# Threshold search of a gated attention block: eight tiles of marks divided anew among ScalarE, VectorE and GpSimd

## What is computed

```python
sim = jnp.einsum('bhnd,bhmd->bnm', Q, K) / (jnp.sqrt(jnp.float32(d)) * H)
k = max(1, int(n * TOP_K_RATIO))                 # 153 of 512
threshold = jax.lax.top_k(sim, k)[0][:, :, -1:]
sparse_mask = (sim >= threshold).astype(sim.dtype)
A_learned = jax.nn.sigmoid(sim) * sparse_mask
A_learned = (A_learned + jnp.swapaxes(A_learned, -1, -2)) * 0.5
x = x + tanh(g_xattn[0]) * ((1.0 - gamma) * layernorm(x) + gamma * A_learned)
```

## Time and profile before

| what | value |
|---|---|
| median of three runs | 1872.8 us (1871.12 to 1873.93) |
| the profiled execution's own time | 1870.53 us |
| its span, first to last instruction | 1868.7 us |
| busy in the span: PE, DVE, ACT, POOL | 1484.8, 1112.7, 980.8, 635.6 us |
| the threshold search | from 41 to about 347 us of the span |

### The profile page before, as it was taken

One profiled execution on the slowest core, in us unless ns is written; L12 is line 12 of the kernel. 1 busy time (PEld: TensorE's weight loads), 2 busy tenths in 40 slices (PEclk: granted clock), 3 DMA queues, 4 the chain that ended last, 5 costly groups with the idle time before them and its releaser, 6 DMA issues. The chain is left out here.

```text
span 1868.7 us, 31243 instructions
## 1 busy us (share of the span) xinstructions
PE 1484.8 (79%) x10376; PEld 777.9 (42%) x10395; DVE 1112.7 (60%) x1785; ACT 980.8 (52%) x1503; POOL 635.6 (34%) x557
## 2 busy tenths in 40 slices
PE   6666666677776775999999711899999999999994
PEld 2444455543333332444444310444444444444442
DVE  3999999788888896888886472205415140541000
ACT  4999999733232233777777440344444444444442
POOL 3000000010000000788888535435445444544432
PEclk9778777788898897999999765999999999999998
DMA  9311100000000000000000256315335151531113
GB/s 336 135 46 46 46 1 1 29 1 1 0 0 0 0 0 1 3 2 3 2 3 3 88 190 249 117 35 163 111 86 168 26 165 34 163 95 34 30 28 102
DMA packets 49246, 118.69 MB, mean 64 GB/s; under 512 B 5536, under 2 KB 5792, under 8 KB 48576
## 3 DMA queue, kind: packets, MB, share of 16 engines
q1 hardware_dynamic: 34832, 88.53, 14.0%
q0 software_dynamic: 8176, 18.65, 5.1%
q10 hardware_dynamic: 6144, 10.28, 1.8%
HBM read 84.21 MB, written 37.43 MB: 65 GB/s over the span
## 5 line engine op out<-in xcount | busy, mean ns | idle before, releaser
L1622 PE MATMUL PS<-R 128*128 (+1 forms) x1872 | 432.7, 381 | 8.3 <-issue 7.2
L1776 DVE TENSOR_SCALAR R<-wring 128x1024 f16<-128x1024 f32 x56 | 61.5, 1108 | 382.6 <-PE PS L1645 349.2
L425 ACT ACTIVATE R<-R 128x512 bf16<-128x512 f32 x448 | 278.9, 715 | 9.4 <-PE PS L445 3.9
L1622 PEld LDWEIGHTS PS<-R 128*128 128x128 f16 x1872 | 179.5, 98 | 217.6 <-issue 19.7
L445 PE MATMUL PS<-R,ident_b 128*128 128x256 bf16 (+1 forms) x1056 | 168.6, 321 | 83.1 <-ACT R L425 79.1
L1645 PE MATMUL PS<-R 128*128 (+1 forms) x936 | 214.8, 379 | 1.2 <-ACT R L1732 1.2
L1812 POOL TENSOR_TENSOR R<-R 128x512 f32<-128x512 f32 x78 | 113.3, 1453 | 292.0 <-ACT R L1720 181.0
L871 PE MATMUL PS<-R 128*128 128x512 bf16 x495 | 141.9, 436 | 78.6 <-DVE R L807 60.4
L1036 DVE TENSOR_REDUCE R<-PS 128x1 f32<-128x512 f32 x256 | 166.6, 686 | 45.2 <-PE PS L1218 42.6
L1014 POOL TENSOR_TENSOR R<-R 128x512 f32<-128x512 f32 x128 | 166.6, 1302 | 27.8 <-ACT R L1141 12.2
L1141 ACT ACTIVATE R<-PS 128x512 f32<-128x512 f32 x256 | 144.4, 598 | 41.3 <-PE PS L1232 40.8
(11 more groups left out here) (262 smaller groups left out, 2522.3 us busy)
## 6 DMA issues: line engine op xcount, KB each, us to landing
wring<-in_L_ffn_w_kernel_dram SPq DMA_DIRECT2D x48, 512.0 KB, 5.3
slot_rows<-R SPq DMA_DIRECT2D x1, 10023.0 KB, 40.3
R<-slot_rows ACTq DMA_DIRECT2D x39, 257.0 KB, 2.7
R<-in_L_ffn_w_kernel_dram SPq DMA_DIRECT2D x16, 512.0 KB, 5.6
wring<-in_L_ffn_wo_kernel_dram SPq DMA_DIRECT2D x16, 512.0 KB, 4.5
R<-in_L_ffn_wo_kernel_dram SPq DMA_DIRECT2D x16, 512.0 KB, 4.7
X<-in_x_dram SPq DMA_DIRECT2D x4, 1024.0 KB, 9.0
R<-in_L_ffn_w_up_dram SPq DMA_DIRECT2D x4, 1024.0 KB, 10.3
```

The costliest lines, as they stand in the source:

```text
L425: nc.scalar.activation(marks[:, j * S:(j + 1) * S], SIM[:, tile * S:(tile + 1) * S], ACT.Sign, bias=cfloat[:, tile:tile + 1], scale=-1.0). ...
L1622: mm = nc.tensor.matmul(bank[2 * half + g], ZT[n][:, (4 * pz + k) * P:(4 * pz + k + 1) * P], weights(place, at), start=(i % 12 == 0), stop ...
```

## The change

ACT makes six of the eight tiles of marks, POOL the last two (`POOL_MARKS = 2`), DVE none. POOL's loop `pool_search` takes the place of `pool_linear`: in each half it waits for the candidates and for the last fold of the half before, marks two tiles, and in every fourth half also does one of the 16 tiles of the linear update. PE's doubled fold covers tiles 6 and 7 and waits for POOL's count; the plain one covers tiles 4 and 5. Two small DVE steps, keep (L513) and near (L536), are written with two tensors as inputs: the constant -1 comes from a new tensor `minus` of 128 x 8 set once by a memset, and the bit, one value per row, is broadcast over the eight columns. The two counting halves behind the search keep their marks on DVE, with the semaphore's counts adapted.

```diff
-ACT_MARKS = 7
+ACT_MARKS = 6
+POOL_MARKS = 2
...
+        minus = R3[:, 5944:5952]
...
                         pe.wait_ge(marked, h * ACT_MARKS + (ACT_MARKS if q else 4))
                         if q:
-                            pe.wait_ge(marked_dve, h + 1)
+                            pe.wait_ge(marked_pool, (h + 1) * POOL_MARKS)
                     else:
-                        pe.wait_ge(marked_dve, HALVES + (h - HALVES) * HALF + 4 * q + 4)
+                        pe.wait_ge(marked_dve, (h - HALVES) * HALF + 4 * q + 4)
                     if q and h < HALVES:
-                        fold((7, 8), ident_2)
-                        mm = fold((4, 7), ident_b[:])
+                        fold((ACT_MARKS, 8), ident_2)
+                        mm = fold((4, ACT_MARKS), ident_b[:])
...
+            nc.vector.memset(minus, -1.0).then_inc(bit_step, 1)
...
-            def mark(h):
-                t = h % 2 * HALF + HALF - 1
-                v.wait_ge(cand_ready, h + 1)
-                if h:
-                    v.wait_ge(fold_ps, 2 * h)
-                nc.vector.tensor_scalar(marks[:, (HALF - 1) * S:], SIM[:, t * S:(t + 1) * S], cfloat[:, t:t + 1], 0.5,
-                                        ALU.is_lt, ALU.subtract).then_inc(marked_dve, 1)
-
...
-                nc.vector.tensor_scalar(keep[:, g], cnt[:, g], float(S - 2 * TOPK), -1.0, ALU.is_le,
-                                        ALU.mult).then_inc(keep_step, 1)
+                nc.vector.scalar_tensor_tensor(out=keep[:, g], in0=cnt[:, g], scalar=float(S - 2 * TOPK), in1=minus,
+                                               op0=ALU.is_le, op1=ALU.mult).then_inc(keep_step, 1)
...
-                    nc.vector.tensor_scalar(near[:, g], key[:, g], bit[:, n + 2:n + 3], None,
+                    nc.vector.tensor_tensor(near[:, g], key[:, g], bit[:, n + 2:n + 3].broadcast_to([P, HALF]),
                                             ALU.bitwise_xor).then_inc(near_step, 1)
...
-            mark(0)
             for u in range(12):
                 for k in range(5):
-                    mark(5 * u + k + 1)
                     search(5 * u + k)
                     dve_weights(v, u, k)
...
-        def pool_linear(pool):
-
-            pool.wait_ge(coef_ready, 5)
-            for t in range(NT):
-                xt = X[:, t * D:(t + 1) * D]
-                nc.gpsimd.tensor_scalar(xt, xt, s1[:, t:t + 1], s2[:, t:t + 1], ALU.mult, ALU.add).then_inc(lin, 1)
+        def pool_search(pool):
+            pool.wait_ge(sim_sb, NT)
+            for h in range(HALVES):
+                pool.wait_ge(cand_ready, h + 1)
+                if h:
+                    pool.wait_ge(fold_ps, 2 * h)
+                for j in range(ACT_MARKS, HALF):
+                    tile = h % 2 * HALF + j
+                    nc.gpsimd.tensor_scalar(marks[:, j * S:(j + 1) * S], SIM[:, tile * S:(tile + 1) * S],
+                                            cfloat[:, tile:tile + 1], 0.5, ALU.is_lt, ALU.subtract).then_inc(marked_pool, 1)
+                if h % 4 == 3:
+                    t = h // 4
+                    if t == 0:
+                        pool.wait_ge(coef_ready, 5)
+                    xt = X[:, t * D:(t + 1) * D]
+                    nc.gpsimd.tensor_scalar(xt, xt, s1[:, t:t + 1], s2[:, t:t + 1], ALU.mult, ALU.add).then_inc(lin, 1)
```

More of the change, by code:

```diff
@@ L97, in bass_flamingo @@
         ln_step = sem("ln_step"); bit_step = sem("bit_step"); cand_ready = sem("cand_ready")
-        marked = sem("marked"); marked_dve = sem("marked_dve"); tallied = sem("tallied"); keep_step = sem("keep_step"); key_step = sem("key_step"); near_step = sem("near_step"); fold_ps = sem("fold_ps"); fin_step = sem("fin_step")
+        marked = sem("marked"); marked_dve = sem("marked_dve"); marked_pool = sem("marked_pool"); tallied = sem("tallied"); keep_step = sem("keep_step"); key_step = sem("key_step"); near_step = sem("near_step"); fold_ps = sem("fold_ps"); fin_step = sem("fin_step")
         tg_ready = sem("tg_ready")
@@ L486, in dve_a @@
             nc.vector.memset(cbits, 0).then_inc(bit_step, 1)
+            nc.vector.memset(minus, -1.0).then_inc(bit_step, 1)
             for n in range(32):
                 nc.vector.memset(bit[:, n:n + 1], -2 ** 31 if n == 0 else 2 ** (31 - n)).then_inc(bit_step, 1)
-            v.wait_ge(bit_step, 35)
+            v.wait_ge(bit_step, 36)
             v.wait_ge(id_ready, 2)
@@ L492, in dve_a @@
             nc.vector.tensor_scalar(ident_2, ident_b[:], 2.0, None, ALU.mult).then_inc(bit_step, 1)
-            v.wait_ge(bit_step, 36)
+            v.wait_ge(bit_step, 37)
             nc.vector.tensor_copy(gone, key).then_inc(cand_ready, 2)
@@ L547, in dve_a @@
             for h in range(60, HALVES):
-                if h + 1 < HALVES:
-                    mark(h + 1)
                 search(h)
@@ L1868, in _ @@
             pool_ln(pool, 0)
-            pool_linear(pool)
+            pool_search(pool)
             pool_b_weights(pool)
```

## The result

The changed kernel takes 2036.9 us against 1872.0: 1.0879 times as long (95% interval 1.0845 to 1.0913), 165 us more. One of the four executions of the changed kernel was slow as a whole (2234.4 us at a granted clock of 0.75) and the ratio leaves it out; the other three took 2032.9 to 2038.4. The kernel before was timed anew beside each group of experiments, with medians from 1872.0 to 1874.5, and each ratio is taken against those times. The forecast had the sign right and nothing else: 1898, with a range of 1860 to 1920.

What follows compares the result with a forecast made beforehand. ACT and DVE, both full, bound the search at 23.9 us a round. DVE's 21.9 plus 4.4 lost to POOL gives 26.3, +28.9 over twelve rounds; less gains at the ends, net +25.4: 1898 us, range 1860 to 1920.

Steps and rivals of the forecast that it cites:

- Part 1 and 2: Search: ACT loses one mark of seven, 3.1 us a round, to 20.8; DVE loses its mark, 2.0, to 21.9.
- Part 3: Small DVE steps (L513, L536) rewritten with two tensors as inputs: same cost, together nothing.
- Part 4, first term: POOL's marks in the search priced at 0.76 us each; with the updates 8.5 us a round.
- signs of being wrong: Closing list: the prediction would be wrong if the marks' instruction is far from 0.76, or DVE comes to wait for folds.
- Part 4, who waits: Search: DVE steps with SBUF inputs and POOL instructions take turns; DVE's loss makes the round 26.3 us against 23.9.
- The loss of 4.4 us: DVE's time lost a round of the search to POOL's marks and updates, between bounds of 2.1 and 7.0.
- lower bound of 2.1: DVE's loss a round if everything that can hide does: 6.4 of POOL's 8.5 us covered by tallies, reduction and reciprocal.
- the placing half by half: POOL's marks placed in each half of a round: DVE losses of 0.15, 2.2 and 1.4 us, plus 0.65 for the update.
- Rival 3: POOL starves behind DVE's train of instructions; mark and fold come on top, 10.6 us a round, 1972 us; chance 0.06.
- 2.0 x 12 + 3.5: Sum of the rival with no blocking to speak of between POOL and DVE: 27.3 us less, 1845.5; chance 0.05.

Runs made afterwards that it cites:

- pool_fast: The changed kernel with POOL's marks computed as mult and add in place of less-than and subtract (not the reference's result): 1868.9 us, 0.9967 of before.
- act7_pool1: The changed kernel with seven tiles of marks on ACT, one on POOL and none on DVE: 1871.0 us, 0.9988 of before.
- narrow_weights: The changed kernel with DVE's weight steps on 64 of each unit's 2048 columns (not the reference's result): 1939.3 us, 1.0354 of before.
- linear_alone: The kernel before with only POOL's linear update moved into the search, one tile every fourth half: 1873.7 us, 0.9995 of before.
- forms: The kernel before plus six POOL instructions of 128x512 while POOL and DVE are idle: mult+add 0.69 and 0.70 us, less-than+subtract 2.02 and 2.00.
- forms2: The kernel before plus six further POOL instructions of 128x512 to bf16 while POOL and DVE are idle: mult alone took 1.57 us.

## Why the prediction was wrong

- **Part 1 and 2** (ACT 20.8, DVE 21.9 us a round; relief of one is worth nothing) fit what was measured: in pool_fast DVE sets the round, in act7_pool1 ACT does, at its 23.9.
- **Part 3** holds: nothing within what can be measured.
- **Part 4, first term: the step that failed.** "The nearest row is the linear update itself, one input, 512 elements, 0.76 us; I take it for the marks." Same engine, same shape, same number of tensor inputs, but another pair of operations: 2.0 us. The price was given without a second end, though the trace had no POOL instruction with this pair; that a mark far from 0.76 would break the sum stands only among the signs of being wrong, with no time worked out for it. With 2.0 the forecast's own fold and the hand-over of 0.13 seen since give the loop: 0.13 + 4.0 + 1.94 is 6.1 us a half before any waiting, against 4.8 available. This loop of marks and fold was never worked out; with 0.76 it would have been 3.6 and harmless.
- **Part 4, who waits.** The sum lets DVE pay for each meeting. In the changed kernel it is POOL that pays: in four halves of five the second mark falls behind one of DVE's long steps and takes 1.5 to 1.8 us more, and in one of them (the half with L721) the first mark is 0.97 longer as well; as POOL is on the loop, everybody waits. narrow_weights puts 98 us on DVE's long steps, some 90 of them on this wait. Which DVE instructions hold POOL's up and which don't was placed rightly (long steps do, tally and reduction don't); that POOL's hold up DVE's two-input steps came true for marks of 0.70 us (L525) and not for those of 2.0.
- **The loss of 4.4 us** with marks of the assumed price was too high as well: 1.7, under the lower bound of 2.1. DVE loses mostly at the candidates (L525, 0.22 a half on average), and little at its long steps, because a mark released in a long step waits until its end and then runs beside the tally, as linear_alone shows with the update alone. The bound of 2.1 had 11.25 x 0.76 in it; with the 0.70 of the pair to bf16 the same sum gives 11.25 x 0.70 - 6.4 = 1.5, and 1.7 lies just above it. What was too high is the step from the bound to 4.4, the placing half by half.
- **Rival 3** (POOL starves, mark and fold on top, 1972) comes nearest in mechanism: POOL does wait for DVE and PE for POOL. It had the loop, but reached it by starvation alone and with the wrong mark. It had 0.06. Two of the rivals' sums are slightly off: 4 x 2.7 is 10.8 a round and not 10.6, which gives rival 3 about 1975, and 2.0 x 12 + 3.5 is 27.5 and not 27.3.
- **The Trainium skill** (SBUF — State Buffer, Who interferes with whom) was right that DVE's two-input steps and a reading POOL instruction contend: L525's 446 ns in pool_fast show it for a one-input POOL instruction. That the loser "fully blocks" for the whole instruction isn't what a mark of 2.0 us shows: two-input steps issued 0.6 and 0.8 us into it took 0.17 and 0.23 us.

Not settled: in narrow_weights 5.2 us a round times twelve is 62 of the 67 us, and in the changed kernel it is 161 of 165. The few that are left lie outside the twelve rounds and were not placed.

## What to carry to other kernels

Price an instruction that moves to another engine by a row of that engine with the same operations, not only the same shape; if there is none, keep both ends open, and work the loop out with the dear one. Give the work to an idle engine only if its longest instruction, its wait for a shared resource and the hand-over still fit into the period of the loop in which it is put. Where two engines are both full, see first whether relieving both is within reach: here even marks of 0.70 us on POOL gained only 0.3%.

## What was not expected of the hardware

- A POOL tensor_scalar of 128x512 takes 0.70 us with mult+add or add+mult, 1.57 with mult, subtract or less-than alone, 2.0 with less-than+subtract, subtract+mult, mult+max or max+min, all with bf16 output (forms, forms2); mult+add and less-than+subtract took the same with 32-bit float output. Adding an operation can make it more than twice as fast: mult alone 1.57, mult+add 0.70.
- A running slow mark is itself held up by a one-input DVE step that starts in its middle. The changed kernel's timeline, one half with such a step:

```profile
282.09 2.96 POOL L599 TENSOR_SCALAR R<-R 128x512 bf16<-128x512 f32 x1 [2.18 <-PE PS L447]
...
283.37 1.22 DVE L721 TENSOR_SCALAR R<-R 128x2048 f32<-128x2048 f32 x1
```

  The mark takes 0.97 more than its 2.0 and the DVE step its free 1.22. It isn't always so: L707, a one-input step of 0.20 us, started at 234.91, 1.6 us into a mark of 2.00 (from 233.28), and took 0.41, to the mark's end; L717, which at 240.24 starts about when a mark that had waited gets to work, takes 1.60 for 1.23. What decides between these cases is open.
- A subtraction of two tensors on POOL with one of them broadcast took 1.04 us, where the subtraction of one value per row took 1.58 and, followed by a product, 2.01.
